# A decoder layer with a non-local block: a second head of four turned by VectorE and through DRAM, and the DMAs of a slot in another order

## The reference

```python
ln_out = layernorm(hidden_states, ln1_s, ln1_b)
q, k, v = jnp.split(ln_out @ w_qkv + b_qkv, 3, axis=-1)
x = hidden_states + merge_heads(attention(q, k, v, ltor_mask)) @ w_ao + b_ao
ln_out = layernorm(x, ln2_s, ln2_b)
q = ln_out @ w_q + b_q
k, v = jnp.split(encoder_states @ w_kv + b_kv, 2, axis=-1)
x = x + merge_heads(attention(q, k, v, cross_mask)) @ w_co + b_co
ln_out = layernorm(x, ln3_s, ln3_b)
x = x + gelu(ln_out @ w1 + b1) @ w2 + b2
...
def attention(q, k, v, mask):
    scores = jnp.einsum('bhqd,bhkd->bhqk', q, k) / jnp.sqrt(jnp.float32(HD))
    scores = scores * mask - 10000.0 * (1.0 - mask)
    return jnp.einsum('bhqk,bhkd->bhqd', jax.nn.softmax(scores, axis=-1), v)
```

## Time and profile before

| what | value |
|---|---|
| median of 3 runs | 2120.47 us |
| lowest and highest of them | 2114.42 and 2125.18 us |
| the profiled execution | 2126.38 us |
| its span | 2124.4 us |
| TensorE (PE) busy | 2010.5 us, 95% |
| VectorE (DVE) busy | 1474.8 us, 69% |
| ScalarE (ACT) busy | 1158.1 us, 55% |
| GpSimd (POOL) busy | 553.4 us, 26% |
| DMA packets | 670396, 257.42 MB, mean 121 GB/s |
| packets under 512 bytes | 483073 |

### The profile page before, as it was taken

One profiled execution on the slowest core, in us unless ns is written; L12 is line 12 of the kernel. 1 busy time (PEld: TensorE's weight loads), 2 busy tenths in 40 slices (PEclk: granted clock), 3 DMA queues, 4 the chain that ended last, 5 costly groups with the idle time before them and its releaser, 6 DMA issues. The chain is left out here.

```text
span 2124.4 us, 41981 instructions
## 1 busy us (share of the span) xinstructions
PE 2010.5 (95%) x13584; PEld 1589.6 (75%) x13584; DVE 1474.8 (69%) x3874; ACT 1158.1 (55%) x3239; POOL 553.4 (26%) x562
## 2 busy tenths in 40 slices
PE   9998999999998999999999999799999999999998
PEld 8876676766766666767777767577888888888887
DVE  7798888987978877977988988566343544434333
ACT  4387777877867877877877877532111111212111
POOL 1022221221224334233333334134131303213100
PEclk9999999999999999999999999899999999999999
DMA  8445565565466665566566566552212121121201
GB/s 273 152 97 124 131 165 124 118 161 126 117 179 159 174 167 140 154 166 140 154 169 152 146 169 155 134 167 65 65 50 68 49 79 37 67 72 51 62 23 45
DMA packets 670396, 257.42 MB, mean 121 GB/s; under 512 B 483073, under 2 KB 614785, under 8 KB 670209
## 3 DMA queue, kind: packets, MB, share of 16 engines
q1 hardware_dynamic: 670208, 255.12, 46.4%
HBM read 170.56 MB, written 84.41 MB: 120 GB/s over the span
## 5 line engine op out<-in xcount | busy, mean ns | idle before, releaser
L1323 ACT ACTIVATE A_p<-A_p,A_nmax 128x256 f32<-128x256 f32 x1024 | 506.6, 500 | 1.7 <-DVE A_res L1591 1.7
L1615 DVE TENSOR_TENSOR A_p<-A_sc,A_mk 128x1024 f32<-128x1024 f32 x256 | 312.2, 1220 | 156.2 <-DMA exponentials<-A_p 80.6
L1625 DVE CUSTOM_DVE_ANT_0 A_p<-A_p,A_ma 128x256 f32<-128x256 f32 x1024 | 372.9, 418 | 4.7
L836 POOL TENSOR_TENSOR A_ct_l<-A_cx,A_ct_h 128x256 fp32r<-128x256 f32 x128 | 118.7, 927 | 725.7 <-DVE A_nmax L1625 694.6
L1330 ACT ACTIVATE A_pt<-A_tp 128x512 f32<-128x512 f32 x384 | 214.3, 589 | 124.8 <-PE A_tp L1085 124.0
L1085 PEld LDWEIGHTS A_tp<-A_ident,A_p 128*128 128x128 f32 x1536 | 185.7, 148 | 77.2 <-issue 32.3
L1085 PE MATMUL A_tp<-A_ident,A_p 128*128 128x128 f32 x1536 | 231.6, 290 | 1.1 <-DVE A_xt_l L1574 0.7
L1103 PE MATMUL A_banks<-A_pt,A_v 128*32 128x256 f32 x2048 | 151.3, 417 | 78.0 <-DMA A_pt<-exponentials 76.5
L1323 ACT ACTIVATION_READ_ACCUMULATOR A_p<-A_p,A_nmax 128x1 f32 x1024 | 196.9, 192 | 0.0
L1462 ACT ACTIVATE A_mk<-A_tp,A_cols 128x512 f32<-128x512 f32 x62 | 42.7, 689 | 269.0 <-PE A_tp L70 269.0
L1462 ACT ACTIVATE A_ma<-A_tp,A_cols 128x512 f32<-128x512 f32 x62 | 42.8, 690 | 241.4 <-PE A_tp L70 241.4
(11 more groups left out here) (247 smaller groups left out, 5074.2 us busy)
## 6 DMA issues: line engine op xcount, KB each, us to landing
exponentials<-A_p SPq DMA_DIRECT2D x512, 64.0 KB, 2.2
A_pt<-exponentials SPq DMA_DIRECT2D x128, 256.0 KB, 3.8
A_x<-x SPq DMA_DIRECT2D x96, 256.0 KB, 3.8
A_res<-x SPq DMA_DIRECT2D x64, 256.0 KB, 2.9
A_rt<-inverses SPq DMA_DIRECT2D x512, 32.0 KB, 1.9
x<-A_res SPq DMA_DIRECT2D x64, 256.0 KB, 3.4
turned<-A_x SPq DMA_DIRECT2D x240, 64.0 KB, 2.2
inverses<-A_turned_inv SPq DMA_DIRECT2D x512, 1.0 KB
```

What stands on the lines that cost most here:

```text
L836: pool.tensor_tensor(ct_l[:, f, part], cx[:, :], f32(ct_h[:, f, part]), ALU.subtract).then_inc(c_lo, 1)
L1323: act.activation(p[:, g % 2, j, t, :], p[:, g % 2, j, t, :], ACT.Exp, scale=-1.0, bias=nmax[:, g % 2, j, t:t + 1], accum_out=rsum[:, g % 2 ...
L1615: dve.tensor_tensor(p[:, g % 2, heads, :, :].rearrange("p j t s -> p j (t s)"), sc[:, heads, :], m, ALU.mult)\
L1625: dve.tensor_tensor_reduce(out=a_, in0=a_, in1=ma[:, b, t, :], scale=-1.0, scalar=BIG, op0=ALU.add, op1=ALU.min, accum_out=nmax[:, g % 2, ...
```

## The change

`MOVED` is 2 and `TURNS` 2: two heads of four are transposed by VectorE and go through DRAM, so the tensor `exponentials` and each of its stores and loads hold twice as much, 128 KB a store and 512 KB a load. The other two are transposed by TensorE at the start of its slot; none is left in the middle. ScalarE computes the first four exponentials of a group ahead of its copies, where it was the first two. The order inside `rsum` changes to head by head, `turned_inv` is stored whole by one DMA with the unused columns too, and the loads pick the wanted pieces of 64 elements in place of 128. The multiplication in `scaled` reads and writes through views in that order. On SyncE `load_res` of slot 6 goes from before the exponentials to the end of the slot, and the two row stores of slot 5 go to slot 6, ahead of it.

```diff
--- before.py
+++ after.py
@@ -25,7 +25,7 @@
 CI = 128
 EPS = 1e-5
 BIG = 3.0e38
-MOVED = 1
+MOVED = 2
 TURNS = HPG - MOVED
 DMA = 16
 
@@ -216,7 +216,7 @@
         rstd = room.sb("rstd", [P, TT])
         nmean = room.sb("nmean", [P, TT])
         nmax = room.sb("nmax", [P, 2, HPG, TPB])
-        rsum = room.sb("rsum", [P, 2, TPB, HPG])
+        rsum = room.sb("rsum", [P, 2, HPG, TPB])
         rinv = room.sb("rinv", [P, 2, 32])
         turned_inv = room.sb("turned_inv", [P, 2, 32])
         shifted = room.sb("shifted", [P, 4, KT])
@@ -528,19 +528,18 @@
 
                 grp, _, g = group(r, h, -1)
                 wait_apart(sp, inv_t, grp + 1, ld_i, (grp - 1) * HPG * DMA)
-                for n in range(P // 32):
-                    sp.dma_start(inv_dram[g % 2][:, n * 32:(n + 1) * 32], turned_inv[n * 32:n * 32 + TPB * HPG, g % 2, :])\
-                        .then_inc(st_i, DMA)
+                sp.dma_start(inv_dram[g % 2], turned_inv[:, g % 2, :]).then_inc(st_i, DMA)
 
             def load_inverses(r, h):
 
                 grp, _, g = group(r, h, -1)
-                wait_apart(sp, st_i, (grp + 1) * (P // 32) * DMA, cx_ok, grp)
+                wait_apart(sp, st_i, (grp + 1) * DMA, cx_ok, grp)
+                blocks = inv_dram[g % 2].rearrange("(n c) s -> n (c s)", c=32).rearrange("(a n) s -> a n s", a=1)
                 for j in range(HPG):
                     rr = slice(j * HD, (j + 1) * HD)
-                    own = inv_dram[g % 2].rearrange("(t j) s -> j t s", j=HPG)[j:j + 1]
-                    sp.dma_start(rt[rr, :].rearrange("p (t s) -> p t s", t=TPB), own.broadcast_to([HD, TPB, P]))\
-                        .then_inc(ld_i, DMA)
+                    own = blocks[:, :, j * TPB * 32:(j + 1) * TPB * 32]
+                    sp.dma_start(rt[rr, :].rearrange("p (n s) -> p n s", n=P // 32),
+                                 own.broadcast_to([HD, P // 32, TPB * 32])).then_inc(ld_i, DMA)
 
             def store_exponentials(r, h):
 
@@ -623,9 +622,6 @@
                 if own:
                     load_exponentials(r, h, pv)
                     store_inverses(r, h)
-                    if h == 6 and 0 < k < NU:
-                        for t in range(2):
-                            load_res(k - 1, r - 1, t + 2)
                 if exists(k, h, 0):
                     store_exponentials(r, h)
                 if own:
@@ -670,22 +666,21 @@
                     load_pair(k - 1, r - 1, 1)
                 if by_blocks(k) and h in (5, 6):
                     load_pair(k, r, h - 5)
-                if by_blocks(k) and h == 4:
-                    store_tile(k, r, 0)
-                    store_tile(k, r, 1)
-                if by_blocks(k) and h == 5:
-                    store_tile(k, r, 2)
                 if k == NU - 1 and h == 1:
                     sp.wait_ge(res_ok, NB * TT)
                     sp.dma_start(ln_scale, across(ln_s)).then_inc(ld_ln, DMA)
                     sp.dma_start(ln_shift[:, :], across(ln_b)).then_inc(ld_ln, DMA)
                 for n in load_at.get((k, h), ()):
                     load_chunk(n)
-                if h == (5 if k < NU else 3) and k:
+                if h == (6 if k < NU else 3) and k:
                     for t in range(2):
                         store(k - 1, r - 1, t)
-                if by_blocks(k) and h == 5:
-                    store_tile(k, r, 3)
+                if by_blocks(k) and h in (4, 5):
+                    store_tile(k, r, 2 * h - 8)
+                    store_tile(k, r, 2 * h - 7)
+                if h == 6 and 0 < k < NU:
+                    for t in range(2):
+                        load_res(k - 1, r - 1, t + 2)
                 if h == (7 if k < NU else 5) and k:
                     for t in range(2):
                         store(k - 1, r - 1, t + 2)
@@ -1321,7 +1316,7 @@
                 if n == 0:
                     wait(act, inv_ok, grp - 1)
                 act.activation(p[:, g % 2, j, t, :], p[:, g % 2, j, t, :], ACT.Exp, scale=-1.0,
-                               bias=nmax[:, g % 2, j, t:t + 1], accum_out=rsum[:, g % 2, t, j:j + 1]).then_inc(exped, 1)
+                               bias=nmax[:, g % 2, j, t:t + 1], accum_out=rsum[:, g % 2, j, t:t + 1]).then_inc(exped, 1)
 
             def turned_out(r, h, i):
                 grp, _, g = group(r, h, -1)
@@ -1629,9 +1624,9 @@
             def inverses(r, h):
                 grp, _, g = group(r, h, -1)
                 dve.wait_ge(exped, (grp + 1) * HPG * TPB)
-                dve.reciprocal(rinv[:, g % 2, 0:TPB * HPG], rsum[:, g % 2, :, :].rearrange("p t j -> p (t j)"))\
+                dve.reciprocal(rinv[:, g % 2, 0:TPB * HPG], rsum[:, g % 2, :, :].rearrange("p j t -> p (j t)"))\
                     .then_inc(inv_ok, 1)
-                wait_apart(dve, inv_ok, grp + 1, st_i, (grp - 1) * (P // 32) * DMA)
+                wait_apart(dve, inv_ok, grp + 1, st_i, (grp - 1) * DMA)
                 dve.transpose(turned_inv[:, g % 2, :], rinv[:, g % 2, :]).then_inc(inv_t, 1)
 
             def exponentials_in_blocks(r, h):
@@ -1646,7 +1641,9 @@
                 dve.wait_ge(done, pv[1])
                 dve.wait_ge(ld_i, (grp + 1) * HPG * DMA)
                 wait(dve, c_lo, grp)
-                dve.tensor_tensor(cx[:, :], banks[:, pv[0], 0:S], rt[:, :], ALU.mult).then_inc(cx_ok, 1)
+                in_order = lambda ap: ap.rearrange("p (t n s) -> p t n s", t=TPB, n=P // 32)
+                dve.tensor_tensor(in_order(cx[:, :]), in_order(banks[:, pv[0], 0:S]),
+                                  rt[:, :].rearrange("p (n t s) -> p t n s", t=TPB, n=P // 32), ALU.mult).then_inc(cx_ok, 1)
 
             def context_low(n):
                 dve.wait_ge(ctx_hi, n + 2)
@@ -1899,7 +1896,7 @@
 
 def decoder_layer_and_nonlocal(nc, a, out):
     m1t = nc.dram_tensor("m1t", [B, P, S], F32, kind="Internal").ap()
-    inverses = nc.dram_tensor("inverses", [2, TPB * HPG, P], F32, kind="Internal").ap()
+    inverses = nc.dram_tensor("inverses", [2, P, 32], F32, kind="Internal").ap()
     exponentials = nc.dram_tensor("exponentials", [2, MOVED, TPB, S, P], F32, kind="Internal").ap()
     turned = nc.dram_tensor("turned", [H, TOK], F32, kind="Internal").ap()
     x1 = nc.dram_tensor("x1", [B, S, H], F32, kind="Internal").ap()
```

## The result

The changed kernel takes 2303.93 us (median of 4 runs, 2296.92 to 2306.81) against 2122.82 for the kernel before on the same chip: a ratio of 1.085, 95% interval 1.082 to 1.089. The forecast was 2130 with a range up to 2195, so the prediction was wrong, too low by 174 us. The profiled execution has 2306.16 us and a span of 2304.2.

A forecast was written before the change was run, and what follows sets the result against it. Ordinary slots were taken as bound by TensorE, one slot a pass by SyncE's DMA list, with VectorE the bound after. Passes netted 0, first slots +5, last pass +5: +10 on the profiled 2126.38 us, forecast 2130, range 2050 to 2195.

The forecast's parts named there:

- TensorE's and VectorE's terms: Attention slots: TensorE loses 0.44 us a slot (56 us), VectorE gains 0.6 (77 us) and becomes the bound.
- The DMA work: Exponentials' stores and load in each slot: 1.43 us added for stores, 0.9 for the load, 2.3 us a slot.
- The share of some 85%: DMA engines in the attention: 18 us a pass added to a share of 0.58 to 0.63, making them some 85% busy.
- Slots 0 to 4 ... 46.1 us after: VectorE in slots 0 to 4: 45.15 us less 2.1 of waits plus 5 x 0.6 gives 46.1 us.
- the flat 2.2 us for an issue of four: SyncE issuing a slot's four stores of exponentials: pieces cost little, 2.2 us against 1.94 today.
- The +10: Whole execution: 5 us for the first eight slots plus 5 for the last pass, with 0 over 15 passes.
- The new wait for `res`: VectorE in slot 7: res and its bias follow the row stores and arrive late, a new wait of 1.9 us.
- rival D: Slot 7: row stores land later, 2 us more a pass, 2160 us; within the forecast case's chance of 0.45.
- The whole order: SyncE's new order: SyncE 3.3 to 4.3 us behind at slot 6 instead of 7.9, slot 6 10.4 us instead of 15.4.
- The reciprocals: SyncE: one DMA for four saves 1.0 us of issuing a slot; pieces half as long on return taken at 0.
- Rival B: Slots 5 to 7: stores keep up and waits go, 2045 to 2078 us, 2060 in the middle; chance 0.30.
- Rival C: Slots 2, 4, 5, 6: store issue takes twice as long, round trip paces the slot, 2175 to 2220 us; chance 0.25.

The follow-up runs named there:

- reciprocals_alone: Kernel before with only the reciprocals' part of the change, one store for four and loads in pieces of 256 bytes, one head through DRAM: 2099.29 us, ratio 0.990.
- long_pieces: Changed kernel storing the same bytes with each partition's row in one contiguous 4 KB piece instead of 32 pieces of 128 bytes: 2231.91 us, ratio 1.051.
- other_heads_first: Changed kernel with VectorE's two masks exchanged, heads 2 and 3, which no store reads, first: 2311.32 us, ratio 1.090.
- no_head_moved: Kernel before with MOVED = 0, all four heads turned by TensorE and no exponentials through DRAM: 2102.02 us, ratio 0.992.

## Why the prediction was wrong

The runs give a ladder, each step one edit: kernel before 2119 to 2121; reciprocals in one DMA 2099 (-20); second head turned by VectorE instead of TensorE, its DMA left out 2122 (+22); its DMA 2252 (+130); SyncE's new order 2304 (+52). The steps depend on their place: the exchange costs 7 us under the new order, the DMA 162, and the order 20 to 52. And the work of the DMA engines by the page (share of the queue times the span):

| kernel | us | work of 16 engines, us |
|---|---|---|
| no head moved | 2102 | 0.312 x 2099.0 = 655 |
| before | 2121 | 0.464 x 2124.4 = 986 |
| reciprocals alone | 2099 | 0.490 x 2098.0 = 1028 |
| second head not moved, old order | 2122 | 0.482 x 2115.9 = 1020 |
| two heads, long pieces, old order | 2162 | 0.531 x 2152.8 = 1143 |
| two heads, old order | 2252 | 0.618 x 2249.5 = 1390 |
| the change | 2304 | 0.603 x 2304.2 = 1389 |

Up to about 1030 us of work the time does not follow it; from there to 1390, in the old order, it rises by 130. The last two rows have the same work and differ by 52 us, so the work alone doesn't set the time.

- **TensorE's and VectorE's terms: the mechanism was right.** A slot with its own DMAs alone is VectorE's, 9.5, 9.4 and 8.6 us for slots 2 to 4 (forecast 9.6, and 8.5 to 9.6 for slot 4). VectorE's busy time in the attention rose by 73 us (forecast 77). TensorE's fell by 6, not by 56: its transposes took 61 less, and the rest took longer, at a granted clock of 0.93 for 0.96. TensorE's waits for VectorE in the exchange alone are the 27.8 and 26.0 us above, against 1.9 and 4.1 in `reciprocals_alone`. The sum had slots 0 to 4 lose 0.95 us a pass by the exchange (45.15 to 46.1), 14 us over 15 passes, and the first eight slots 5; alone it costs 22.
- **The DMA work was sized 20% low, 2.3 us a slot for 2.9.** (1390 - 1020) / 128 = 2.9: the stores (1250 - 1011) / 128 = 1.87 for 1.43 (1250 = 0.564 x 2216.2, 1011 = 0.473 x 2138.2), the load (1389 - 1250) / 128 = 1.09 for 0.9. The share of some 85% was forecast and 0.77 and 0.83 came, partly by luck: both the work and the pass were longer than forecast.
- **The step that failed** is "Slots 0 to 4 ... 46.1 us after", a sum of VectorE's work with no DMA wait in it, together with the flat 2.2 us for an issue of four. Slots 0 and 1 carry row loads, row stores and loads of `res`; they took 11.7 and 10.8 us, all five 49.95. The price of 2.2 us was taken as a property of the DMA, and here it went with what else the queue carried: 2.24 in light slots, 3.55 to 4.91 in crowded ones. By the same error slot 5 began with SyncE 5.0 us behind (549.72 - 544.69) where I had 3.2, slots 5 and 6 came out 2.8 and 2.5 us longer than forecast, and slot 7 3.3. These and the 3.9 of slots 0 to 4 make 12.4 us over the forecast in this pass. Between VectorE's first masks, the 14 passes after the first are each 9.4 to 15.5 us longer than before, 170 us together, where the sum had 0: nearly all of the 174 that were missed. (The +10 that it had for the first slots and the last pass came out at 1.) A mean share of some 85% was given no wait in slots 0 to 4, when it is the mean of light slots at 0.62 to 0.66 and crowded ones at 0.77 to 0.93, slots 0 and 1 among them.
- **The new wait for `res`** came in slot 7 and was forecast at 1.9 us; it measured 3.47 there and 50.9 us over 15 passes. That is rival D, 1.6 us more a pass, and explains little of the miss. The sum saw that SyncE is held too and had VectorE's longer slot hide it. SyncE's wait is 59.9 us at L497, with the next slot's load and reciprocals queued behind it (576.69 follows 575.61), and TensorE then stands 3.26 us for the load in slot 7. Both waits went together with the row stores' place, so how the 30 us divide between them is not shown. The whole order was to shrink slot 6 by relieving SyncE; it costs 52 us.
- **The reciprocals** were put at nothing: 20 us less with one head, nothing with two. In the change as a whole the term held.
- **Rival B** (the stores keep up) fell. The formula in the Trainium skill, "DMA: Bandwidth & Descriptors", "Anatomy of one DMA", 2.0 us and the bytes at 436 GB/s, has no term for pieces or for other traffic and was fitted to DMAs that GpSimd issues. By it, as an estimate, a 128 KB store lands in 2.3 us. The measured median is 3.6, and `long_pieces` gets 249 us of engine time back from the same bytes. The measurement decides.
- **Rival C** (the round trip paces the slot, 2175 to 2220) was nearest in time, still 84 us too low, and half right. Its sign came: the first masks of slots 0, 1 and 2 wait 0.43, 2.18 and 1.25 us for stores of exponentials. Issuing takes twice as long, but in slots 5, 6, 7, 0 and 1 (3.55 to 4.91 us) and not in 2 and 4 (2.24 and 2.25), which it named. That the chain blocks, store, landing, mask sets the pace isn't so: slack for the mask in `other_heads_first` changed nothing. The rival held to one chain, while TensorE's load, the reciprocals and `res` come late in the crowded slots too.

Not settled: how the 52 us of the order split beyond the 30, and why it costs 36 with one head turned on TensorE and 20 with the second on VectorE; why long pieces and the old order together give 18 us more than apart; how the cost of the DMA divides between the engines' time and the blocked issues; and whether the blocked issues follow the engines' time or the number of pieces, since both fell together in `long_pieces`.

## What to carry to other kernels

Before adding DMA work, take the share of the DMA engines stretch by stretch, not as a mean, and add the new work to the slots that already have neighbours on the queue: here the slots at 0.77 to 0.93 were late, those at 0.62 to 0.66 were not, and a price of issuing read in a quiet slot doubled in the crowded ones. If a wait for a DMA only moves elsewhere when its consumer is shifted, with its sum nearly unchanged, look to what delays all the DMAs of that slot: here taking work off the queue helped (the load 89 us, long pieces 72), and shifting the consumer did not. And ask of a path through DRAM what it saves at one unit less: here the kernel with none, which gives TensorE more to do, beats the kernel before by 0.8%.

## What the runs showed of the hardware

- The same four DMAs take 2.24 us to issue on SyncE in a slot with its own DMAs alone and 4.91 soon after 1 MB of row loads (595.55 to 599.47); a single issue then holds SyncE for up to 2.6 us in this pass and 3.8 in the whole attention, and everything behind it.
- 325.98 MB in 533171 packets take 1140 us of the 16 engines, in 1041074 packets 1389 us: 249 us x 16 engines for 507,903 packets more is 7.8 ns of one engine for each.
- TensorE's granted clock rose to 1.00 over both stretches of the attention where it waited for no exponentials (`no_head_moved`), against 0.96 before and 0.93 to 0.94 after; 1.00 is the level of 2.4 GHz, and the lower values are means that mix in the 1.2 GHz level. The stalled slot 6 itself had 0.79, slots 6 and 7 of the pass above 0.85 and 0.90, but its slots 5, 0 and 1 had 1.00 in spite of their waits. So the clock was lower where TensorE had stalled and not where it had most work, though not after every stall. The same 16 matmuls took 1.94 us behind the stall of slot 6 and 1.07 a slot later, so a stall may cost more than its own length; how much in all was not measured apart.
